# First layer of a graph network: the turned one-hot matrix made by ScalarE in two steps instead of by VectorE in one

## What is computed

```python
h = relu(layernorm(x))
s, v = h[:, :64] @ W_nl0, einsum('nmi,mk->nki', h[:, 64:].reshape(N, 32, 3), W_nl1)
w = relu(edge_feature @ W_fc1) @ W_fc2          # 64 -> 64 -> 224, per edge
xs, xv = s[dst], v[dst]                          # rows of the destination nodes
# five kinds of products of w, xs, xv and the edge's direction -> 480 numbers per edge
agg = segment_sum(tp, src, num_segments=N) / 32
x = x + gated(agg @ W_out + skip)
```

## Time and profile before

| | |
|---|---|
| median of 3 runs | 8548.7 us (8541.74 to 8609.48) |
| profiled execution, its own time | 8655.61 us |
| its span | 8653.9 us |
| granted TensorE clock over the span | 0.884 |
| span, TensorE / VectorE / ScalarE / GpSimd busy | 83 / 79 / 39 / 58% |

### The profile page before, as it was taken

How to read it: one execution, slowest core, us unless ns; L and a number is a source line. 1 busy time by engine, 2 the same in 40 slices (tenths; PEclk the granted TensorE clock), 3 DMA queues, 4 the chain that set the end, 5 groups by cost and what they waited for, 6 DMA issues and landing times. The chain is left out here.

```text
span 8653.9 us, 111370 instructions
## 1 busy us (share of the span) xinstructions
PE 7204.2 (83%) x32226; PEld 4840.7 (56%) x32226; DVE 6840.9 (79%) x20357; ACT 3363.3 (39%) x8451; POOL 4980.2 (58%) x4078
## 2 busy tenths in 40 slices
PE   3999999993899999699999947788888888886567
PEld 1444444443455455445544537677777777775455
DVE  5999999994677777577777748778887878787895
ACT  1444444441333233323332325455555555554000
POOL 0777777770566666267766517667767667662000
PEclk9999999995799999689999958888998988898796
DMA  4999999993122222022222112222222222221342
GB/s 163 162 165 169 168 166 168 167 156 117 54 56 57 55 57 56 24 57 61 60 58 59 51 33 67 71 72 75 77 77 72 75 74 75 73 71 47 107 140 80
DMA packets 459615, 776.94 MB, mean 90 GB/s; under 512 B 96641, under 2 KB 310886, under 8 KB 458758
## 3 DMA queue, kind: packets, MB, share of 16 engines
q0 software_dynamic: 274944, 469.50, 28.0%
q1 hardware_dynamic: 178166, 299.52, 11.0%
q10 hardware_dynamic: 5904, 0.79, 0.1%
HBM read 464.60 MB, written 304.85 MB: 89 GB/s over the span
## 5 line engine op out<-in xcount | busy, mean ns | idle before, releaser
L588 POOL DMA_INDIRECT fore<-node_table,src_i x1664 | 1766.6, 1062 | 961.2 <-issue 494.8
L1332 DVE TENSOR_TENSOR work<-work 128x384 f32<-128x384 f32 (+4 forms) x4726 | 1784.7, 406 | 198.5 <-ACT work L922 91.4
L628 POOL DMA_INDIRECT src_sum<-work,put_i x832 | 1323.6, 1591 | 621.8 <-ACT work L812 455.5
L1146 PE MATMUL bank<-work 128*128 128x384 f32 (+1 forms) x3328 | 1359.7, 557 | 94.0 <-DVE work L1332 72.6
L588 POOL DMA_INDIRECT fore<-src_table,src_i x784 | 924.7, 1179 | 820.2 <-DVE work L1332 407.0
L1332 DVE TENSOR_TENSOR work<-work,y 128x384 f32<-128x384 f32 (+2 forms) x2548 | 970.6, 431 | 374.5 <-ACT work L934 248.0
L1146 PEld LDWEIGHTS bank<-work 128*128 128x128 f32 x3328 | 674.5, 213 | 859.5 <-issue 416.0
L588 POOL DMA_INDIRECT fore<-dst_table,dst_i x784 | 943.8, 1204 | 238.9 <-issue 238.9
L1332 DVE TENSOR_TENSOR work<-work,bank 128x384 f32 (+6 forms) x2080 | 896.8, 431 | 154.9 <-remote 73.6
L824 ACT ACTIVATE work<-bank 64x512 f32<-64x512 f32 x416 | 246.0, 591 | 1801.1 <-PE bank L1113 1101.0
L1072 PE MATMUL bank<-work 128*128 128x480 f32 x1664 | 782.1, 605 | 3.1 <-DVE work L1332 2.9
(11 more groups left out here) (240 smaller groups left out, 12777.6 us busy)
## 6 DMA issues: line engine op xcount, KB each, us to landing
edge_h<-work SPq DMA_DIRECT2D x196, 320.0 KB
work<-edge_h SPq DMA_DIRECT2D x196, 320.0 KB, 2.8
work<-keys SPq DMA_DIRECT2D x196, 256.0 KB
fore<-node_table,src_i POOLq DMA_INDIRECT x1664
work<-in_edge_attr SPq DMA_DIRECT2D x196, 128.0 KB
src_sum<-work SPq DMA_DIRECT2D x4, 6240.0 KB, 41.1
work<-src_sum SPq DMA_DIRECT2D x100, 240.0 KB, 3.3
src_sum<-work,put_i POOLq DMA_INDIRECT x832
```

What stands on the lines that cost most here:

```text
L588: return pool.indirect_dma_start(dst, None, table, bass.IndirectOffsetOnAxis(ap=idx, axis=0), bounds_check=bound, oob_is_err=True)
L628: pool.indirect_dma_start(src_sum[t], bass.IndirectOffsetOnAxis(ap=put_i[:, e:e + 1], axis=0), E.run[:, g % 2, t * 480:(t + 1) * 480], Non ...
L1146: last = nc.tensor.matmul(o, W.sel[:, b, t, :], W.msg[:, b, t * f:(t + 1) * f], start=t == 2 * i, stop=t == 2 * i + 1)
L1332: return V_.tensor_tensor(o, p, q, op)
```

## The change

VectorE's keys_by_place is removed. ScalarE gets a stage of the same name, three groups ahead and last in its list: for each of the four tiles |place - key| into a new scratch tile E.away, then, after all four, relu(1 - away) over all four tiles into E.turned, which is 1 where the key is the place and 0 elsewhere. Its bias of one is a new column, unity. SyncE loads the keys with lag 0 rather than -2 and waits also until ScalarE has read the buffer; edges() now waits for the keys itself.

```diff
@@ SyncE, edge_keys
                     sp.wait_ge(s.keys_read, g - DEPTH + 1)
+
+                    sp.wait_ge(s.turned_keys, g - DEPTH + 1)
@@
-            unrolled(ALL_GROUPS, [(-2, edge_keys), (0, edge_scalars)])
+            unrolled(ALL_GROUPS, [(0, edge_keys), (0, edge_scalars)])
@@ ScalarE
+            def keys_by_place(g):
+                b = g % 2
+                act.wait_ge(keys_in[g % DEPTH], arrived(g, DEPTH))
+                if g >= 2:
+                    act.wait_ge(s.rows_mm, g - 1)
+                if g:
+                    act.wait_ge(s.turned_keys, g)
+                for t in range(GROUP):
+                    u = 2 * g + t // 2
+                    act.activation(E.away[:, t, :], E.keys[:, g % DEPTH, t, 1, :], ACT.Abs, bias=place[:, u:u + 1],
+                                   scale=-1.0).then_inc(act_own, own.step())
+                act.wait_ge(act_own, own.n)
+                act.activation(E.turned[:, b], E.away, ACT.Relu, bias=unity[:], scale=-1.0).then_inc(s.turned_keys, 1)
@@
-            unrolled(ALL_GROUPS, [(0, run_out), (-2, fc_out), (-3, relu_out)])
+            unrolled(ALL_GROUPS, [(0, run_out), (-2, fc_out), (-3, relu_out), (-3, keys_by_place)])
+            act.sem_inc(act_own, own.reset())
@@ VectorE
+            V_.memset(unity[:], 1.0).then_inc(dve_own, c.step())
@@
-            def keys_by_place(g):
-                b = g % 2
-                dve.wait_ge(keys_in[g % DEPTH], arrived(g, DEPTH))
-                if g >= 2:
-                    dve.wait_ge(s.rows_mm, g - 1)
-                for t in range(GROUP):
-                    u = 2 * g + t // 2
-                    last = V_.tensor_scalar(E.turned[:, b, t, :], E.keys[:, g % DEPTH, t, 1, :], place[:, u:u + 1], None, ALU.is_equal)
-                last.then_inc(s.turned_keys, 1)
@@ edges
                 own_keys = src_f[:, g * GROUP:(g + 1) * GROUP]
+
+                dve.wait_ge(keys_in[g % DEPTH], arrived(g, DEPTH))
                 if g >= 2:
                     dve.wait_ge(s.run_mm, GROUP * (g - 1))
@@
-            unrolled(ALL_GROUPS, [(-2, keys_by_place), (0, edges)])
+            unrolled(ALL_GROUPS, [(0, edges)])
```

More of the change, by code:

```diff
@@ L136, in build @@
         place = sb("place", [P, UNITS + MORE])
+        unity = sb("unity", [P, 1])
         put_i = sb("put_i", [P, ALL_TILES], I32)
@@ L260, in edge_views @@
             v.turned = g(2, GROUP, P)
+            v.away = g(GROUP, P)
             v.run = g(2, GROUP * 480)
```

## The result

The changed kernel takes 8719.2 us (median of 4 runs, 8688.66 to 8788.4) against 8567.0 for the kernel before in the same comparison (4 runs, 8541.74 to 8609.48): **1.0175 of it, 95% interval 1.0133 to 1.0217**, 152 us slower. The direction was forecast; the size was not: 344 us (8893 us) was forecast, and 8719 lies just above the lower end of the range (8710). The profiled execution has a span of 8786.7 us against 8653.9.

The account below looks back on a forecast made before the run. VectorE, TensorE and DMA were all read near their end at 8.29 us a group. TensorE's 7.85 + 1.39 = 9.24, at clock 0.90 9.95 us; 8548.7 + 344 = 8893 us, range 8710 to 9060.

Parts of the forecast that it names:

- Where ScalarE's steps stand, and that they stall TensorE: First layer's edge loop: steps between ReLU and first run_out delay TensorE's third product of the sums by 1.39 us.
- The sizes of the five steps: ScalarE, each group: four Abs 1.27 us, wait on itself 0.06, ReLU 0.73; run_out starts 2.55 us after the sums.
- table load: Rival, chance 0.02: Abs and ReLU in different tables, two loads of 1.283 us a group on ScalarE; over 9270 us.
- TensorE's own chain: TensorE's serial work in a group (sums, weights, rows, weights, hidden) without the attribute wait: 7.85 us.
- The term of the clock: TensorE's granted clock in the first layer's edge stage falls from 0.99 to 0.90, taking a group from 9.24 to 9.95 us.
- clock holds: Rival, chance 0.22: same TensorE stall but full clock, 9.24 us a group, +197 us, 8746 us.
- SyncE's part: Keys at lag 0 no longer hold up the attributes; TensorE's wait for them, 0.34 us a group, goes.
- VectorE's relief: VectorE loses four comparisons, 0.86 us a group, its path 0.8; alone a gain of at most 60 us.
- 72% as a sign: Sign of being right: VectorE's busy share in the first layer's edge stage falls to about 72%.
- Its ceiling: Limit on the gain from fewer VectorE comparisons: DMA packets, 0.97 x 8.29 = 8.0 us a group.
- The faster rival: Chance 0.05: ScalarE's steps cost TensorE nothing since the sums start late; DMA bounds at 8.0 us a group, 8489 us.

Follow-up runs that it names:

- e1_between: Changed kernel with ScalarE's five new steps moved between the two halves of fc_out, nothing else: 7917.4 us, 0.985 of the kernel before.
- e3_gap_one: Changed kernel with one extra ScalarE output of 128x512, which nothing reads, between its two new steps: 1.0311 of the kernel before.
- e4_gap_two: Changed kernel with two extra ScalarE outputs, which nothing reads, between its two new steps: 1.0462 of the kernel before.
- e8_thin_sums: Changed kernel with the products of the sums cut from 480 to 160 columns, scatter bytes kept: 1.096 of the kernel before, one run.
- e10_keys_ahead: Changed kernel with SyncE loading the keys two groups ahead again (lag -2): 8237.1 us, 1.0198 of the kernel before.
- e6_sync_only: Kernel before with SyncE's part of the change alone (keys at lag 0), comparisons left on VectorE: 7914.7 us, 0.9941 of the kernel before.
- e12_vector_too: Changed kernel with VectorE doing its four comparisons as well, into a place nothing reads: 8253.4 us, 1.0216 of the kernel before.
- e11_changed_again: The changed kernel, unchanged, run again on another chip as yardstick: 8237.7 us, 1.0209 of the kernel before.

## Why the prediction was right and wrong

- **Where ScalarE's steps stand, and that they stall TensorE: right.** run_out starts 2.52 us after the sums (forecast 2.55, and 2.4 to 2.7 as the sign). e1_between shows that it is the place and nothing else.
- **The sizes of the five steps: right.** Four Abs 1.26 us (1.27), the ReLU 0.72 (0.73), the wait of ScalarE on itself 0.03 (1007.00 + 1.26 to 1008.29; I took 0.06). TensorE's second pair of products starts 3.13 us after the sums (1009.53 - 1006.40); with 1.79 before the change (1008.28 - 1006.49 in the earlier trace rows) and the forecast 1.39 more, 3.18 was forecast. The 0.03 is idle time alone: where ScalarE doesn't wait for itself, the next instruction starts some 0.1 before the last one ends, and that overlap is gone too. There is no room for a table load between the two steps, so that rival is out.
- **TensorE's own chain: 7.85 taken, 7.78 measured** (e1_between), so 7.78 + 1.34 = 9.12 for a group, where I had 9.24 at a full clock.
- **The term of the clock: wrong, the step that made the prediction wrong.** I let the granted clock fall to 0.90 for a stall of 1.4 to 1.6 us, on one row of another stage, and added 9.95 - 9.24 = 0.71 us a group, 147 us of the 344. It is 1.00 here. Without that term the sum is 197 us more and 8746 us, the rival "clock holds", to which I gave 0.22, against 152 us more and 8719 measured (170 us more in the stage itself). I had put the fall down to the length of the stall, on a row of another stage that doesn't show this by itself; e3_gap_one (1.77 us, clock 1.00) and e4_gap_two (2.29 us, 0.99) show that a stall even longer than the forecast one leaves the clock all but alone in this stage, and e8_thin_sums, in one run, that the work around the stall counts there.
- **SyncE's part: right as to where, its worth depends on the rest.** The attribute wait is gone. Under the new stall that is worth nothing (e10_keys_ahead), in the kernel before it is worth 0.6% (e6_sync_only), which I hadn't priced by itself (23 us of it seen in the stage).
- **VectorE's relief: right that it earns nothing in the change** (e12_vector_too). VectorE's busy share came out at 83%, where I gave 72% as a sign: the group is shorter than I took it, and the work a group fell from 8.18 to 7.52 us (busy share times the group) and not by the whole 0.86. Its ceiling was wrong: I capped it at 8.0 us a group by the DMA engines' 0.97 and forecast a share of 0.8 after. It reads 0.94 with 10% less traffic, and e1_between goes to 7.82 us. That cap was a misreading of the share and had no part in the forecast time.
- **The faster rival** needed run_out not to be due when the steps run. In the change it is due; with the same work between the halves of fc_out it isn't (e1_between).

The group loses 0.82 us (9.11 against 8.29) and not the whole 1.34 of the later start, because the kernel before wasn't at TensorE's 7.78 but at VectorE's 8.2 and the waits for the attributes. TensorE's chain had 0.5 us to spare under these, and the later start uses that up first. It isn't VectorE's relief that gives the 0.5 us back: with the comparisons still on VectorE (e12_vector_too) the group is 9.10 us all the same.

## To carry to other kernels

An engine with half its time free has that time at certain places of its queue: before giving it work, look in one period in order of time at where the other engines' waits on it fall due, and put the work into the gap before them; here the same instructions are worth +1.8 to +2.1% in one place and -1.3 to -1.5% in another. A clock term can't be taken from another stage by the length of one stall alone: look at what else the engine did around that stall, and where the work there isn't like the work at hand, forecast without the term and give it as a rival. A DMA share near 1 isn't a wall by itself; one run with more traffic tells.

## What I had not expected of the hardware

- TensorE kept all but its full clock with a stall of 2.29 us in each 10.2 us (0.99; slower products behind one stall in 19), and stood at the lower level for most of the stage with stalls of 1.70 and 2.32 us once the products of the sums were thinned from 480 to 160 columns (0.55, one run).
- The DMA share of a stretch goes above one (1.04 at 177 GB/s, 1.03 at 198), and for the same changed kernel at the same 152 GB/s it reads 0.94 in one profile and 0.98 in another, on another chip (e11_changed_again); e10_keys_ahead, on that second chip, reads 0.94 again. Why, wasn't tried.
- A wait of ScalarE on its own semaphore between two dependent steps leaves 0.03 us idle. Without a wait two steps overlap by 0.09 us (e3_gap_one, below), so it costs some 0.12 us.

```profile
1004.03 0.63 ACT L813 ACTIVATE fore<-work 128x512 f32<-128x512 f32 x1
1004.57 0.71 ACT L815 ACTIVATE work<-work,unity 128x512 f32<-128x512 f32 x1
```
